# Row sends reordered, one dense step in front, and nine products of a constant tile, in a two-layer gated cross-attention and expert kernel

## The reference

```python
x = x + tanh(g_xattn[0]) * cross_attention_one_head(ln(x), ctx, Wq, Wkv)
x = x + tanh(g_ffn[0])   * expert_choice_attention(ln(x), Wr, Wqkv, Wo)   # 8 experts, 64 tokens of each batch
x = x + tanh(g_xattn[1]) * cross_attention_16_heads(ln(x), ctx, ctx, mask, Wq, Wk, Wv, Wo)
x = x + tanh(g_ffn[1])   * top2_experts(ln(x))
```

## Time and profile before

| | |
|---|---|
| median of 3 runs | 321.09 us (319.01 to 323.36) |
| profiled execution | 319.61 us, of it 317.8 us span |
| busy: PE, DVE, ACT, POOL | 84%, 74%, 64%, 50% |
| granted TensorE clock, mean | 0.941 of full speed |

### The profile page before, as it was taken

One profiled execution on the slowest core, in us unless ns is written; L12 is line 12 of the kernel. 1 busy time (PEld: TensorE's weight loads), 2 busy tenths in 40 slices (PEclk: granted clock), 3 DMA queues, 4 the chain that ended last, 5 costly groups with the idle time before them and its releaser, 6 DMA issues.

```text
span 317.8 us, 7526 instructions
## 1 busy us (share of the span) xinstructions
PE 268.3 (84%) x2406; PEld 201.9 (64%) x2406; DVE 236.4 (74%) x711; ACT 204.4 (64%) x469; POOL 158.9 (50%) x206
## 2 busy tenths in 40 slices
PE   7878986997999797999988853878899999999950
PEld 4553442555677464676766732368799999999940
DVE  3586198857977666788999967998576767677796
ACT  2964799796577588976855543535657575756560
POOL 2624297024622546643024777770047878787531
PEclk9999999899999999999999655879999999999995
DMA  7890003001269999970000011113122223111064
GB/s 211 233 383 10 1 2 132 0 3 19 117 188 185 178 181 180 190 105 0 2 1 24 30 45 40 53 49 88 37 71 68 78 67 87 51 32 33 8 226 132
DMA packets 34612, 28.12 MB, mean 88 GB/s; under 512 B 3072, under 2 KB 32389, under 8 KB 33936
## 3 DMA queue, kind: packets, MB, share of 16 engines
q1 hardware_dynamic: 32192, 23.77, 33.8%
q0 software_dynamic: 2240, 3.72, 3.6%
q10 hardware_dynamic: 144, 0.15, 0.2%
HBM read 14.15 MB, written 14.40 MB: 90 GB/s over the span
## 4 chain that ended last, share of the span: by engine, by line
PE 52%; DVE 30%; ACT 8%; issue 6%; DMA 2%; SPq 1%; POOL 1%; DVEq 0%
PE bank L1195 47%; DVE region_k L912 2%; DVE region_x L1152 2%; DVE top L911 2%; DMA wr<-in 2%; PE bank L1492 1%; DVE bn_raw L870 1%; DVE nm L1001 1%; DVE region_k L1003 1%; DVE x L1141 1%; DVE x L1142 1%; ACT x_hat L540 1%; DVE x L902 1%; PE bank L1419 1%; DVE region_k L969 1%
## 5 line engine op out<-in xcount | busy, mean ns | idle before, releaser
L1177 DVE TENSOR_TENSOR region_k<-region_x,region_k 128x768 f16<-128x768 f32 (+1 forms) x33 | 30.6, 926 | 21.6 <-ACT region_k L714 21.6
L1195 PE MATMUL bank<-w_high,region_k 128*128 (+1 forms) x380 | 37.8, 221 | 6.4 <-DVE x L1171 3.3
L1195 PE MATMUL bank<-w_scaled,w_high 128*128 128x256 f16 x252 | 42.5, 273 | 0.1
L846 POOL DMA_INDIRECT expert_rows<-region_k,slot_dest x22 | 27.1, 1232 | 26.5 <-DVE region_k L1164 19.2
L714 ACT ACTIVATE region_k<-region_x 128x768 f16<-128x768 f32 (+1 forms) x33 | 26.8, 813 | 15.8 <-DVE region_x L1152 13.7
L820 POOL DMA_INDIRECT dispatched_rows<-region_t,slot x28 | 28.8, 1028 | 16.1 <-issue 8.3
L1195 PEld LDWEIGHTS bank<-w_high,region_k 128*128 128x128 f16 x380 | 30.9, 99 | 7.7 <-issue 7.3
L1195 PE MATMUL bank<-w_scaled,w_low 128*128 128x256 f16 x126 | 34.3, 273 | 0.0
L1195 PE MATMUL bank<-w_low,region_k 128*128 (+1 forms) x190 | 34.0, 221 | 0.0
L1152 DVE SCALAR_TENSOR_TENSOR region_x<-bank,region_w 128x768 f32<-128x768 f32 (+1 forms) x33 | 30.4, 920 | 3.2 <-ACT region_w L719 2.2
L1195 PE MATMUL bank<-filler 128*128 128x512 f16 x94 | 26.9, 407 | 3.9 <-DVE region_k L912 2.4
(11 more groups left out here) (242 smaller groups left out, 736.1 us busy)
## 6 DMA issues: line engine op xcount, KB each, us to landing
dispatched_rows<-pad_rows SPq DMA_DIRECT2D x8, 1048.0 KB, 18.8
w_scaled<-in SPq DMA_DIRECT2D x5, 1024.0 KB, 8.0
w_scaled<-dispatched_rows SPq DMA_DIRECT2D x21, 131.0 KB, 2.3
region_q<-expert_rows SPq DMA_DIRECT2D x3, 512.0 KB, 5.0
x<-in SPq DMA_DIRECT2D x4, 256.0 KB, 4.4
region_w<-in SPq DMA_DIRECT2D x2, 512.0 KB, 7.0
out<-x SPq DMA_DIRECT2D x3, 256.0 KB, 2.3
w_scaled<-in SPq DMA_DIRECT2D x1, 704.0 KB, 4.1
```

The lines of the kernel that those rows point to most:

```text
L846: pool.indirect_dma_start(ytok, bass.IndirectOffsetOnAxis(dst[:, n, h:h + 1].bitcast(U32), 0), yv[n % 4][:, h * D:(h + 1) * D], None, boun ...
L1177: dve.tensor_tensor(hsplit[:, v, k:2 * k], hid[:, v, 0:k], hsplit[:, v, 0:k], ALU.subtract).then_inc(hidden_low, 1)
L1195: return pe.matmul(o, l, r, start=start, stop=stop)
```

## The change

Five things.

1. `DENSE_FIRST` is 1, so one dense step stands in front of the row tiles and seven behind them.
2. On DVE the slots of group 0 move from 15 to 14.25 in the list (from behind `shift 13` to right behind `shift 12`), those of group 1 from 19 to 18.35 (from behind `affine 11` to behind `add 12`).
3. The sends are issued by tile, in four stages `send0` to `send3`, right behind the slots. POOL's list was: send of group 0, `rstd2` of group 2, send2 of group 0, `rstd2` of group 3, send of group 1, `rstd2` of group 4, send2 of group 1, group 2, group 3. It is now: all four tiles of group 0, `rstd2` of group 2, first tile of group 1, `rstd2` of group 3, two tiles of group 1, `rstd2` of group 4, last tile of group 1, group 2, group 3.
4. On PE four products of the tile of ones (128 x 512) stand in front of the ranks of group 2, and five in front of the turn of group 4.
5. In the tail DVE adds only group 0. ACT scales group 2 inside the step loop, behind the silu of the last step and ahead of the last step's high part, then groups 1 and 3 behind the loop; POOL adds groups 2, 1, 3. The loads of `yk` come in the order 2, 0, 1, 3; the stores in the order 2, 0, 1, 3, 4.

```diff
-DENSE_FIRST = 3
+DENSE_FIRST = 1
-C_POOL = {... "rstd2": 6.5, "send": 12.5, "send2": 16.1}
+C_POOL = {... "rstd2": 6.5, "send0": 11.3, "send1": 11.32, "send2": 11.34, "send3": 11.36}
-C_DVE_AT = {("affine", 13): 20.8, ...
+C_DVE_AT = {("slots", 3): 14.25, ("slots", 7): 18.35, ("affine", 13): 20.8, ...
-C_POOL_AT = {("rstd2", 13): 19.4, ("rstd2", 15): 21.5, ("send2", 7): 21.6, ("send", 11): 21.7, ("send2", 11): 21.8, ("send", 13): 21.9}
+C_POOL_AT = {("rstd2", 13): 18.5, ("send0", 7): 18.4, ("send1", 7): 18.6, ("send2", 7): 18.7, ("rstd2", 15): 21.3, ("send3", 7): 21.4,
+             **{(f"send{k}", t): t + 10.5 + 0.1 * k for t in (11, 13) for k in range(4)}}
+FILL_RANK, FILL_TURN = 4, 5
@@ SyncE
-            for g in (0, 2, 1, 3):
+            for g in (2, 0, 1, 3):
                 n = slice(*GROUPS[g])
                 eng.dma_start(yk[:, n, :], ytok_v[:, n, :]).then_inc(x_loaded[g], 16)
-            for g, ready, count in ((2, last_added, 2), (0, sum_done, T), (SPARSE, rows_ready, len(STEPS)), (3, last_added, 4),
-                                    (1, sum_done, 2 * T)):
+            for g, ready, count in ((2, last_added, 2), (0, sum_done, T), (1, last_added, 4), (3, last_added, 6),
+                                    (SPARSE, rows_ready, len(STEPS))):
@@ ScalarE
+            def gated_rows(g):
+                act.wait_ge(gates_done, 1)
+                act.wait_ge(x_loaded[g], 32)
+                for c in range(2):
+                    for t in range(*GROUPS[g]):
+                        last = act.activation(yk[:, t, c * D:(c + 1) * D], yk[:, t, c * D:(c + 1) * D], ACT.Copy,
+                                              scale=gate[:, t, c:c + 1])
+                    last.then_inc(last_gated, 1)
...
+                if s == len(STEPS) - 2:
+                    gated_rows(2)
...
-            for g in (2, 3): ...
+            gated_rows(1)
+            gated_rows(3)
@@ GpSimd
-            def send_rows(tiles_of_group):
-                for t in tiles_of_group:
-                    for c in range(2): ...
+            def send_rows(t):
+                for c in range(2): ...
-                elif stage == "send" and g is not None and g < SPARSE: (waits) send_rows(range(lo, lo + 2))
-                elif stage == "send2" and g is not None and g < SPARSE: send_rows(range(lo + 2, hi))
+                elif stage[:4] == "send" and g is not None and g < SPARSE and lo + int(stage[4]) < hi:
+                    if stage == "send0": (waits)
+                    send_rows(lo + int(stage[4]))
-            for k, (g, c) in enumerate(((2, 0), (2, 1), (3, 0), (3, 1))):
+            for k, (g, c) in enumerate((g, c) for g in (2, 1, 3) for c in range(2)):
@@ VectorE
                 elif s == len(STEPS):
-                    sum_rows(range(1, 4))
-            dve.wait_ge(x_loaded[1], 32)
-            sum_rows(range(4, 8))
+                    sum_rows(range(1, 3))
+            sum_rows(range(3, 4))
@@ TensorE, turn of group 4
+                        pe.wait_ge(cross1_exp_out, NT)
+                        fillers(bank[2][:, :], FILL_TURN)
@@ TensorE, rank
+                    if g == SPARSE - 2:
+                        pe.wait_ge(cross1_exp_out, NT)
+                        fillers(bank[2][:, :], FILL_RANK)
```

More of the change, by code:

```diff
@@ L93 @@
          "route": 10.9, "slots": 12}
-C_POOL = {"rstd": -4.6, "early_low": -5.3, "low": -0.9, "rstd2": 6.5, "send": 12.5, "send2": 16.1}
+C_POOL = {"rstd": -4.6, "early_low": -5.3, "low": -0.9, "rstd2": 6.5, "send0": 11.3, "send1": 11.32, "send2": 11.34, "send3": 11.36}
 C_FIRST = 3
@@ L99 @@
             ("norm2", 15): 21.9, ("high", 15): 22.1, ("turn_out", 15): 22.3}
-C_DVE_AT = {("affine", 13): 20.8, ("low", 13): 21.0, ("route", 11): 21.4, ("slots", 11): 21.6,
+C_DVE_AT = {("slots", 3): 14.25, ("slots", 7): 18.35, ("affine", 13): 20.8, ("low", 13): 21.0, ("route", 11): 21.4, ("slots", 11): 21.6,
             ("affine", 15): 22.0, ("low", 15): 22.1, ("route", 13): 22.2,
             ("route", 15): 22.5, ("slots", 13): 22.9}
-C_POOL_AT = {("rstd2", 13): 19.4, ("rstd2", 15): 21.5, ("send2", 7): 21.6, ("send", 11): 21.7, ("send2", 11): 21.8, ("send", 13): 21.9}
+C_POOL_AT = {("rstd2", 13): 18.5, ("send0", 7): 18.4, ("send1", 7): 18.6, ("send2", 7): 18.7, ("rstd2", 15): 21.3, ("send3", 7): 21.4,
+             **{(f"send{k}", t): t + 10.5 + 0.1 * k for t in (11, 13) for k in range(4)}}
 FILL_LOAD, FILL_NORM, FILL_CROSS, FILL_SELECT, FILL_ROUND = 10, 4, 2, 3, 4
+FILL_RANK, FILL_TURN = 4, 5
 C_ID, C_HM, C_HR, C_S, C_STP, C_EREG, C_I8, C_P8, C_2T = 0, 128, 144, 160, 208, 256, 264, 272, 280
@@ L724, in _ @@
                     act.activation(gone[:, :], gdif[:, :], ACT.Tanh, scale=0.5).then_inc(top2_tanh, 1)
-            act.wait_ge(gates_done, 1)
-            for g in (2, 3):
-                act.wait_ge(x_loaded[g], 32)
-                for c in range(2):
-                    for t in range(*GROUPS[g]):
-                        last = act.activation(yk[:, t, c * D:(c + 1) * D], yk[:, t, c * D:(c + 1) * D], ACT.Copy,
-                                              scale=gate[:, t, c:c + 1])
-                    last.then_inc(last_gated, 1)
+            gated_rows(1)
+            gated_rows(3)
         @block.gpsimd
@@ L813, in _ @@
                                    bcp(c32[:, C_HM:C_HM + H], KC), ALU.mult).then_inc(k_blocks_done, 1)
-            def send_rows(tiles_of_group):
-                for t in tiles_of_group:
-                    for c in range(2):
-                        pool.indirect_dma_start(disp, bass.IndirectOffsetOnAxis(slot[:, t, c:c + 1].bitcast(U32), 0),
-                                                pay[:, t, :], None).then_inc(sent, 16)
+            def send_rows(t):
+                for c in range(2):
+                    pool.indirect_dma_start(disp, bass.IndirectOffsetOnAxis(slot[:, t, c:c + 1].bitcast(U32), 0),
+                                            pay[:, t, :], None).then_inc(sent, 16)
             for stage, t in skewed(NT, C_EVERY, C_POOL, C_POOL_AT):
@@ L831, in _ @@
                     rstd_of(g, ffn_stats, ffn_rstd, (lo, hi))
-                elif stage == "send" and g is not None and g < SPARSE:
-                    pool.wait_ge(padded, 16 * (E + 2))
-                    pool.wait_ge(slots_ready, g + 1)
-                    pool.wait_ge(ffn_high, g + 1)
-                    pool.wait_ge(ffn_low, g + 1)
-                    send_rows(range(lo, lo + 2))
-                elif stage == "send2" and g is not None and g < SPARSE:
-                    send_rows(range(lo + 2, hi))
+                elif stage[:4] == "send" and g is not None and g < SPARSE and lo + int(stage[4]) < hi:
+                    if stage == "send0":
+                        pool.wait_ge(padded, 16 * (E + 2))
+                        pool.wait_ge(slots_ready, g + 1)
+                        pool.wait_ge(ffn_high, g + 1)
+                        pool.wait_ge(ffn_low, g + 1)
+                    send_rows(lo + int(stage[4]))
             for n in range(TILES):
```

## The result

The changed kernel took 327.46 us in the median (322.96 to 329.76, 4 runs) and the kernel before, on the same chip, 320.22 us (319.01 to 323.36, 4 runs). The ratio is 1.0165, with a 95% interval of 1.0099 to 1.0232: slower, by something between 1% and 2.3%, so whether by 2% is not decided. The profiled execution took 327.28 us with a span of 325.4 us, against 319.61 and 317.8.

A forecast was written before the change was run, and what follows sets the result against it. Bounds: GpSimd's sends until the last dispatched row, TensorE from 225 to 302 us, VectorE's adds in the tail. Front +4.7, tail -0.2, products 0 give +4.5 on the profiled 319.61: 324.1 us, range 317 to 329.

The forecast's parts named there:

- half clock behind the stall: TensorE's products after its idle gap before the first row tile: half clock for 3.3 us, costing 1.65 us more.
- First send, 3.7 us earlier: GpSimd in the routing hop: earlier slots of group 0 let the first send begin at 166.7 instead of 170.38.
- Last send at 211.3: End of GpSimd's sends: 211.3 instead of 213.84, after a longer wait for group 1's slots; bounds 210.3 to 213.84.
- The sends end past 213: GpSimd's last send ending after 213 us, named in advance as a sign that the forecast is wrong.
- From the last send to the tile's destinations, 4.92 us: First row tile: it lands as long after the last send as before, 213.84 to 218.76, hence at 216.2.
- VectorE stands in `slot_dest`: First tile's destinations: VectorE waits from 213.0 to 216.2, delaying the shared add to 218.0 and TensorE's down product.
- the second rival: TensorE's clock survives the stall before the first row tiles: 1.65 us less, 322.5 us in all; chance 0.15.
- Front +4.7: Up to the row tiles and steps behind: third turn 1.2 us earlier, two more dense steps of 5.94 us, +4.7.
- The nine products, 0: Constant-tile products on TensorE before group 2's ranks and the last turn: inside idle time, cost 0, gain 0.
- The third rival: Nine products bring TensorE to full clock before the shared steps, on the path: 2.6 us saved, 321.5 us; chance 0.05.
- Tail -0.2: Tail: VectorE's adds -2.8, ScalarE's scalings +1.4, stores +1.1, sum -0.2 us; bounds -2.8 to +2.9.
- the fourth rival: Tail grows by 2.9 us through ScalarE's scalings and GpSimd's added adds: 327.2 us, over 2% slower; chance 0.2.

The follow-up runs named there:

- e11: Changed kernel with one edit, the store of group 0 moved from second to last place: 323.44 us, 1.0033 of the kernel before.
- e10_dest_later: Changed kernel with VectorE's destinations of the first two row tiles put behind the dense step's low part: 323.51 us, 1.0107 of the kernel before.
- e4_b_dense1: Kernel before with one dense step in front instead of three, nothing else changed: 328.83 us, 1.0218 of the kernel before.
- e3_nofill: Changed kernel without the nine products of the constant tile: 325.19 us, 1.0093 of the kernel before.
- e6: Changed kernel with ScalarE's eight scalings of group 2 moved behind the last step: 323.52 us, 1.0095 of the kernel before.
- e12: Changed kernel with two dense steps in front, no nine products, group 2's scalings behind the last step, group 0 stored last: 323.70 us, 1.0033.
- e13: Changed kernel without the nine products, group 2's scalings behind the last step, group 0 stored last, first two tiles' destinations later: 323.57 us, 1.0027.
- e8_dense2_oldtail: Changed kernel with two dense steps in front, the old tail and no nine products: 321.12 us, 1.0000 of the kernel before.
- e14_drain: Changed kernel, two dense steps, no products, later scalings and destinations, group 3 added on VectorE, stores 2, 1, sparse, 0, 3: 322.35 us, 1.0027.

## Why the forecast held, point by point

The forecast was 324.1 us, 317 to 329, no difference of 2% as the likeliest: 327.46 lies in the range, 3.4 us above. In the profiled executions the early stretch, which no step of the forecast speaks of, is 2.6 of these, and front and tail, +4.97 against +4.5, are 0.5. The mechanism, a tile that lands late behind too little cover with VectorE's queue behind it, was right. That the sum came so close is in part luck: half clock behind the stall was put at 1.65 us and did not come, a sag in the hop that the forecast did not have cost 1.5 us, and the tail was missed by 1.2 us.

- **First send, 3.7 us earlier: held** (3.8). Group 1's wait was put at 2.9 us and was 3.25.
- **Last send at 211.3, that is 50.56 behind the anchor: 52.49.** The step that fell short is "All else on it is the same work": it is, but the attention in front of group 1's slots runs on TensorE, and where its clock sags there, the wait grows (2.69 us in e11, 3.25 in after) and the one for group 2's statistics, gone in e11, stays (1.06 us). Where the clock did not sag from 8 to 12 us the last send ended at 49.9 to 51.0, so the forecast lies in the middle of these, and after's end inside the bounds (210.3 to 213.84 are 49.6 to 53.1). "The sends end past 213", which is 52.3 behind the anchor, was a sign of being wrong: after, with 52.49, shows it by 0.2 us, and no execution without the sag does.
- **From the last send to the tile's destinations, 4.92 us: 3.80.** SyncE issued the load 1.58 us behind the last send (217.44 less 215.86) instead of 2.35, a gap that varies between traces, and VectorE was waiting for it; so the tile was used 0.8 us later than forecast, not 1.9.
- **VectorE stands in `slot_dest`, with the shared add queued behind it, and TensorE waits for the add: held**, in the trace (2.04, then 1.48 us) and by e10_dest_later.
- **Half clock behind the stall, 1.65 us: did not happen in after.** This is the second rival, with a chance of 0.15. The gap was 1.38 and 1.48 us with a turn between, and the clock stayed at 2.4 GHz; behind the single gap of 5.50 us in e4_b_dense1 it fell. The earlier trace rows showed a gap of 3.07 us and none of 1 to 2 us, so this could not be read from before.
- **Front +4.7: 3.98, and +2.5 in e11, without the sag.** In after the third turn came 1.9 us earlier instead of 1.2, from +0.8 for the tile, -1.65 for the clock and +0.1 for the rest; two dense steps, 5.94 us, follow as forecast. That this part gains nothing even without a stall fits as well: with waits of only 0.21 and 0.45 us left (e10) the front is 1.3 us over before; the bound had +0.1. (Its own terms, 214.9 and then 2.64 and 1.1 us, give 218.6 and not 218.8, so -0.1.)
- **The nine products, 0: held.** The third rival, their clock on the path, is out by e3_nofill: the clock came back earlier, and the shared add did not. The rule of the Trainium skill on sustained activity (TensorE: Matmul & The Clock Gate, Part 1) agrees with that, 0.93 of the clock against 0.50; the stretch behind the products is not bound by TensorE.
- **Tail -0.2: +0.99.** The terms: VectorE's last add 1.4 us earlier by the sum, 0.84 measured, and the difference is for the most part the wait of 0.53 us for the last down product, which the sum did not have; the stores +1.1 by the sum, and 1.83 measured (2.77 to 4.60 us from the last add to the end), of which the order of the stores explains 1.1 (e11). Beyond the terms there was one that the forecast did not have: GpSimd's drain. In after it ends at 324.1, 1.3 us in front of the end, so it does not set it; but it is the floor on which e11 stops (last addition to 313.5, drain to 319.4, end 319.6) and on which e6, e12 and e13 sit. The forecast's lower bound for the tail, -2.8, could not be reached with GpSimd's two additions more: in after the drain ends 15.5 us behind the last silu, 0.3 under the tail of before. Nor do its terms give it; -0.2 less four collisions of about 1 us is -4.2.
- **As many collisions as before, against two more of the fourth rival: held.** Before, four adds of VectorE took 1.40, 1.37, 0.81 and 0.83 us instead of 0.35 beside GpSimd's adds, 3.0 us too much in all. After, the low part, 0.96 us alone, took 1.64, and three adds took 1.35, 1.36 and 0.79: 3.1 us too much. The Trainium skill has a reason (SBUF — State Buffer, section on the two separate sides: the port pair that VectorE and GpSimd share is an exclusive lock, held for the instruction), and the trace agrees: an add's 1.0 us more, 1.35 against 0.35, is within one GpSimd addition, 1.26 us in the median. The rival's +2.9 in the tail did not happen.

What stays open: how much of the timed 7.2 us is the change. The pair of traces gives 5.0 from the anchor on, 3.5 with e11's front, and the interval of the ratio is 3.2 to 7.4 us; the changed kernel was timed in four runs only. Why TensorE's clock sags in one stretch or another, early and in the hop, in executions of one program was not found, nor why the last sends and the first load's issue vary by 1 us and more.

## What to carry to other kernels

Work that covers a latency is worth its own length and not a microsecond more: before moving it away, count what the path needs when the latency is gone altogether; here even a tile that is there at once left nothing to gain by the forecast's own bound, and the variant with the least waiting was 1.3 us over before in the front. When a wait is placed in an in-order queue, list what stands behind it on that engine: a wait of 1.4 us for a tile became another 1.5 us for an add that had nothing to do with it. Before taking work off the engine that ends last, look for the one that would end last next, the closing drain of GpSimd included, and order the stores by when their data is ready.

## What the runs showed of the hardware

- GpSimd's closing drain ended 5.8 to 5.9 us after the end of its last addition in all 14 traces, before too (311.1 to 317.0), and no span ended before it. The closing drains of the others took 0.4 to 0.8 us (VectorE), 1.1 to 2.1 (TensorE) and 1.3 to 3.5 (ScalarE). In a kernel like this one GpSimd's last computation has to be over 6 us before the end that is wanted.
- Equal programs had TensorE at half clock in different stretches from one execution to the next: 12 to 20 us in after, only 12 to 16 in e8_dense2_oldtail (0.57), not at all in before. The anchor, at 160.0 to 160.9 us where the clock was full from 12 to 20 us and at 161.9 to 164.3 where it was not, moved over 4.2 us, as much as the change is worth, while the executions of one kernel spread by up to 7.7 us. One execution of before, beside e14_drain, fell out of all this: 447.67 us at a mean granted clock of 0.554.
- Stalls of 1.4 and 1.5 us with one turn between them (after) left TensorE at 2.4 GHz; single ones of 5.5 us (e4_b_dense1) and 3.07 us (before) were followed by half clock.
